# First experts' results stored by slot and gathered by token; six of eight images enter the third attention inside its steps

## The chip, the cores and the metric

The kernel runs on one core of a Trainium2 chip (trn2). Its engines work in parallel, each through its own instruction stream, and meet through semaphores: TensorE (PE: matrix products and transposes, results in PSUM), VectorE (DVE), ScalarE (ACT), GpSimd (POOL) and SyncE (SP), which here only issues transfers. GpSimd issues the indirect transfers (gathers and scatters of rows of 128 floats, one row per partition). The metric is the device time of one execution in microseconds; lower is better. Profiled executions give the trace.

## The reference

Eight images of 128 channels and 256 pixels pass through two convolutional attention layers, an attention (L2), a mixture of experts (L2), an attention (L3) and a mixture of experts (L3). What the change touches, cut to it (t is 8 images x 256 tokens x 128):

```python
t = t + _L2_ffn_ref(_ln_t(t), ...)     # first experts: 8 experts of 128 -> 512 -> 128, gelu, biases, top 2 of 8
t = t + _L3_attn_ref(_ln_t(t), ...)    # third attention: 8 heads of 16, 256 x 256 scores for each image and head
t = t + _L3_ffn_ref(_ln_t(t), ...)     # second experts: 8 experts of 128 -> 256 -> 128, silu(x w1) * (x w3), top 2

def _L2_ffn_ref(x, gate_w, gate_b, w1, b1, w2, b2):
    raw_weights = softmax(x @ gate_w + gate_b)
    top_w, top_idx = top_k(raw_weights, 2)
    expert_out = gelu(x @ w1[e] + b1[e]) @ w2[e] + b2[e]     # for each expert e
    return sum of expert_out[top_idx] * top_w                # for each token

def _L3_attn_ref(hidden_states, Wq, Wkv, Wo, bo):
    q, k, v = projections, 8 heads of 16
    scores = (q * scale @ k.T).astype(bfloat16)
    probs = softmax(scores)                                  # bfloat16
    out = (probs.astype(float32) @ v).astype(bfloat16)
    return out.astype(float32) @ Wo + bo
```

## The kernel before

The tokens t lie in SBUF as 128 partitions x (half s of the image, image b, 128 channels); N is 256 tokens of an image, T is 2048. Float32 operands of products are split into a high part (fp32r) made by ScalarE and a low part made by VectorE, and multiplied in three passes (xH*wH, xL*wH, xH*wL).

**First experts**, `experts(0, ...)`, one block of instructions (`nc.Block`; all five engines meet at its end). The router on VectorE and TensorE gives each of the 4096 pairs of token and expert a slot in 39 tiles of 128 rows (NT = 39), each tile of one expert. `pos` holds the slot of each pair; `slots`, `rows_of_slots` and `tables` turn this into `idx`, for each slot the row of the tokens' copy in DRAM (`rows_in`), and `places_aside` into `idy`, the row of `rows_out` where its result goes (rows of empty slots go to a place aside). GpSimd gathers tile j by `idx` into `xg` (`gather(j)`, six buffers), TensorE transposes and multiplies (`transposed`, `up`, `hidden_transposed`, `down`), ScalarE and VectorE evacuate, VectorE writes the result to `yo` (`result(j)`, L1479, three buffers), GpSimd scatters it by `idy` to `rows_out` (`scatter(j)`, L1109). GpSimd's order is: eight gathers, then scatter j and gather j + 8 in turn. After the last scatter has landed, SP fetches `rows_out` in token order into `both` (`fetch`, L946), one pair of images c at a time, two transfers per pair; pairs 0 and 1 in this block, 2 and 3 in the next. `both` is the same memory as `xc` (the first result of each token) and `lnT` (the second).

**Third attention**, `block4`. For each of four pairs of images: ScalarE scales the second results by their gates (`weighted_rows`), VectorE adds both to t (`combine`, L962 and L968), takes mean and variance (`measured`, L203, L208, L895), GpSimd raises the variance to -1/2 (`pair_pool`, L899), VectorE normalises (`pair_apply`, L906), TensorE transposes (`pair_transposes`, L917), ScalarE and VectorE make `xH` and `xL` (`pair_high` L923, `pair_low` L929), TensorE projects the values (`project_values`), ScalarE brings them to `v3f` (`values_out`), and GpSimd splits them into three bf16 parts (`split_values`, L1587 to L1593). All this for all pairs stands in front of, or inside, the first of 32 steps; a step (b, g) works on two of the eight heads of image b. The order inside a step is written out by hand for each engine and staggered: in step (b, g) TensorE makes the scores of three steps ahead, ScalarE rounds those of two steps ahead (`rounded`, L1618) and takes the exponentials of one step ahead (L1627), VectorE takes the maxima and subtracts them one step ahead (`centre`, L1818 to L1823), normalises the present ones (`normalise`, L1828, L1831), takes the low parts of a projection five fragments ahead (`lower`, L1810, L1812) and gathers outputs (L1846, L1854, L1859). `images` runs the steps: image 0 written out, images 1 to 5 as a loop, 6 and 7 written out. PSUM bank 0 (QKB) holds the projections of queries and keys in its two halves, and banks 4 to 7 the values and transposes of the start.

**Second experts**, `experts(1, ...)`: the same code with `hid` 256; its results go by scatter and fetch, and stay so.

## Time and profile before

| | |
|---|---|
| median of 3 runs | 623.33 us (623.15 to 624.60) |
| profiled execution | 623.73 us, span 621.9 us, mean granted clock 0.771 |
| PE / PEld busy | 503.7 us (81%) / 395.8 us (64%) |
| DVE busy | 433.9 us (70%) |
| ACT busy | 284.4 us (46%) |
| POOL busy | 286.1 us (46%) |
| first experts, from block to block | 161.9 to 306.06 us |
| third attention | 306.06 to 469.43 us |

A span is the time from the first to the last instruction of the trace; the device time holds 1.8 us more. Busy shares are means over stages with different limits, so they are read by stage. "PEclk" is the granted clock of TensorE as a share of 2.4 GHz: 0.50 is 1.2 GHz. A timeline row gives start, duration, engine, line and operation, out<-in, how many instructions are merged in it, and in brackets the idle time before it and what ended it.

### The profile page before, as it was taken

What the parts mean: (1) busy time and instruction counts of PE and PEld (TensorE: products, weight loads), DVE (VectorE), ACT (ScalarE), POOL (GpSimd) and SP (SyncE); (2) the same over time, 40 slices, a digit from 0 to 9 for tenths busy, and PEclk for the clock granted to TensorE, in tenths of its full rate; (3) what the DMA queues carried; (4) which work ended last, traced back from release to release, by engine and by line L of the source; (5) the groups of instructions that cost most, each with busy time, mean ns of one, the idle gap of its engine ahead of it and who ended that gap; (6) DMA issues with size and microseconds to landing.
All of it is one profiled execution on the core that took longest, in us unless ns stands there. A gap on an engine that the chain in (4) does not pass through costs nothing. (4 is left out here: it accounts for less than half of the span.)

```text
span 621.9 us, 10346 instructions
## 1 busy us (share of the span) xinstructions
PE 503.7 (81%) x3062; PEld 395.8 (64%) x3062; DVE 433.9 (70%) x1235; ACT 284.4 (46%) x754; POOL 286.1 (46%) x269
## 2 busy tenths in 40 slices
PE   9998995889667999999148899999857668777752
PEld 4785563859534999998147787777647346555531
DVE  2628559998876458544388799999997866555534
ACT  4523134400311764444236899999861023333324
POOL 1093438879344677775112111111112157777750
PEclk9698576999658999999665555555555799999995
DMA  6000070000550111212500000000004011112216
GB/s 226 1 1 2 0 271 0 1 1 1 188 150 26 49 52 52 52 53 43 147 1 2 1 2 0 0 0 0 1 2 114 22 35 51 52 52 51 51 48 199
DMA packets 26508, 31.06 MB, mean 50 GB/s; under 512 B 3105, under 2 KB 21538, under 8 KB 26338
## 3 DMA queue, kind: packets, MB, share of 16 engines
q1 hardware_dynamic: 21474, 20.29, 10.1%
q0 software_dynamic: 4992, 10.23, 6.4%
q8 instruction: 24, 0.39, 0.3%
q14 instruction: 18, 0.15, 0.1%
HBM read 20.16 MB, written 10.36 MB: 49 GB/s over the span
## 5 line engine op out<-in xcount | busy, mean ns | idle before, releaser
L1103 POOL DMA_INDIRECT xg<-rows_in,idx x78 | 76.5, 981 | 36.5 <-issue 21.6
L1109 POOL DMA_INDIRECT rows_out<-yo,idy x78 | 77.0, 988 | 31.8 <-issue 18.3
L1161 ACT ACTIVATE hraw<-ps 128x512 f32<-128x512 f32 (+1 forms) x78 | 38.3, 492 | 94.1 <-PE ps L1271 94.1
L1471 DVE TENSOR_TENSOR hidden<-ps,hidden 128x512 fp32r<-128x512 f32 (+1 forms) x78 | 43.3, 555 | 42.5 <-ACT hidden L1168 42.5
L1292 PE MATMUL ps<-wHL,hidden 128*128 x234 | 68.8, 346 | 0.6 <-DVE hidden L1471 0.4
L1295 PE MATMUL ps<-wHL,hidden 128*128 x234 | 53.9, 230 | 0.0
L1627 ACT ACTIVATE p<-s 128x256 bf16<-128x256 bf16 x128 | 51.6, 413 | 3.5 <-DVE s L1823 3.4
L1587 POOL CAST vp<-v3f 128x256 bf16<-128x256 f32 x8 | 3.6, 450 | 95.8 <-ACT s L1618 95.8
L1292 PEld LDWEIGHTS ps<-wHL,hidden 128*128 128x128 f32 x234 | 44.1, 189 | 2.9 <-issue 1.4
L1154 ACT ACTIVATE xa<-ps 128x128 fp32r<-128x128 f32 x78 | 21.9, 281 | 50.2 <-PE ps L1255 49.7
L1295 PEld LDWEIGHTS ps<-wHL,hidden 128*128 128x128 f32 x234 | 44.6, 191 | 0.0
L1269 PE MATMUL ps<-wHL,xa 128*128 x78 | 34.5, 443 | 10.6 <-issue 9.8
L1479 DVE TENSOR_REDUCE yo<-ps 128x128 f32<-128x256 f32 x78 | 32.6, 418 | 11.4 <-PE ps L1295 8.6
L1466 DVE TENSOR_TENSOR hraw<-hraw,ps 128x256 f32<-128x256 f32 x39 | 16.4, 422 | 33.0 <-ACT hraw L1161 33.0
L1168 ACT ACTIVATE hidden<-ps 128x512 fp32r<-128x512 f32 (+1 forms) x78 | 37.8, 485 | 1.5 <-PE ps L1279 1.5
L1279 PE MATMUL ps<-w,hraw 128*128 128x128 f32 x234 | 38.2, 272 | 0.3 <-DVE hraw L1466 0.3
L1279 PEld LDWEIGHTS ps<-w,hraw 128*128 128x128 f32 x234 | 30.2, 140 | 10.8 <-DVE hraw L1466 0.6
L1712 PE MATMUL ps<-identb,p 128*128 128x128 bf16 x256 | 33.3, 310 | 4.1 <-DVE p L1831 3.6
L763 PE MATMUL ps<-w,pw 128*128 128x128 f32 x256 | 30.7, 285 | 4.4 <-DVE pw L596 4.4
L763 PEld LDWEIGHTS ps<-w,pw 128*128 128x128 f32 x256 | 30.4, 201 | 5.4 <-issue 3.7
L1255 PE MATMUL ps<-w,xg 128*128 128x128 f32 x78 | 22.9, 293 | 13.4 <-DMA xg<-rows_in,idx 12.8
L1618 ACT ACTIVATE s<-ps 128x1024 bf16<-128x1024 f32 x32 | 32.8, 1024 | 1.7 <-PE ps L1701 0.3
(287 smaller groups left out, 1398.6 us busy)
## 6 DMA issues: line engine op xcount, KB each, us to landing
wraw<-in_ex SPq DMA_DIRECT2D x2, 2048.0 KB, 10.1
rows_in<-both SPq DMA_DIRECT2D x8, 512.0 KB, 5.9
both<-rows_out SPq DMA_DIRECT2D x16, 256.0 KB, 4.1
wraw<-in_ex SPq DMA_DIRECT2D x1, 3072.0 KB, 12.7
w<-in_pack SPq DMA_DIRECT2D x1, 1582.0 KB, 8.3
xg<-rows_in,idx POOLq DMA_INDIRECT x78, 2.6
rows_out<-yo,idy POOLq DMA_INDIRECT x78, 2.3
xs<-in_x SPq DMA_DIRECT2D x4, 256.0 KB, 4.6
```

What stands on the lines that cost most here:

```text
L763: x = pe.matmul(o, pw[:, q, k, :], ident, start=k == 0, stop=k == B - 1)
L1103: pool.indirect_dma_start(xg[:, j % NXG, :], None, xs_d[:], bass.IndirectOffsetOnAxis(idx[:, j:j + 1], 0)).then_inc(ld[j % NXG], 16)
L1109: pool.indirect_dma_start(ys_d[:], bass.IndirectOffsetOnAxis(idy[:, j:j + 1], 0), yo[:, j % NYO, :], None).then_inc(st[j % NYO], 16)
L1161: act.activation(hraw[:, j % 2, :], ps[:, HB + j % 2, 0:hid], ACT.Gelu if layer == 0 else ACT.Silu).then_inc(z["act"], 1)
L1168: act.activation(hH[:, j % 2, :], ps[:, HTB + j % 2, 0:hid], ACT.Copy).then_inc(z["hH"], 1)
L1269: pe.matmul(o, xa[:, j % NX, :], wh, start=layer == 1, stop=False)
L1279: x = pe.transpose(ps[:, HTB + j % 2, h * P:(h + 1) * P], hraw[:, j % 2, h * P:(h + 1) * P], ident)
L1292: pe.matmul(o.rearrange("p (i n) -> p i n", i=2), hH[:, j % 2, h * P:(h + 1) * P], both, start=h == 0, stop=False)
L1295: x = pe.matmul(o[:, 0:P], hL[:, j % 2, h * P:(h + 1) * P], wHL[:, bass.ds(e, 1), 0, cols].rearrange("p a n -> p (a n)"), start=False, sto ...
L1471: dve.tensor_tensor(hL[:, j % 2, :], ps[:, HTB + j % 2, 0:hid], hH[:, j % 2, :].bitcast(F32), ALU.subtract).then_inc(z["hL"], 1)
L1627: act.activation(p3[:, g % 2, r, :], s3[:, g % 2, r, :], ACT.Exp, accum_out=smb3[:, g, r:r + 1]).then_inc(m3["ex"], 1)
L1712: x = pe.transpose(psb(TB)[:, ((h * S + kt) * S + s) * P:((h * S + kt) * S + s + 1) * P], p3[:, g % 2, h * S + s, kt * P:(kt + 1) * P], id ...
```

## The change

First experts: `scatter` and `idy` are gone in this layer. VectorE copies `pos` to `slot_of`; SP stores each result tile as it is to `rows_by_slot`, in slot order; GpSimd issues all gathers of tokens, waits for all stores, and then gathers the results of image 0, four indirect transfers of 128 rows (`result_rows`: two halves of the image, two experts). The results of images 1 to 7 are gathered by GpSimd in the next block, four transfers an image.

Third attention: the work of the start is done image by image instead of pair by pair (`add_rows`, `scaled_rows`, `image_sum`, `image_apply`, `image_transposes`, `image_high`, `image_low`, `image_values`, `image_values_out`, `image_pool`). Images 0 and 1, and sum and normalisation of image 2, stand before the steps. The rest of image 2, and images 3 to 7, stand in the steps: with n = 4b + g, image i is summed in step n = 4i - 10, normalised one step later, transposed two, split into high and low part three, its values projected three and brought out four steps later (`coming`). The transposes and values use the half of bank 0 that the projection of the same step doesn't. `images` is written out in full, without a loop. The transfers of images 1 to 3 are mixed by hand on GpSimd with the powers of images 0 to 2 and the splitting of the values.

```diff
+        def image_pool(pool, b):
+            pool.wait_ge(c3["var"], b + 1)
+            pool.tensor_tensor(rstd[:, :, b], var[:, :, b], halfs[:, 0:S], ALU.pow).then_inc(c3["rst"], 1)
+
+        def image_sum(dve, b):
+
+            add_rows(dve, b)
+            ln_moments(dve, chv, range(S), (b,))
+            chv.wait()
+            dve.tensor_scalar(var[:, :, b], mv[:, :, b, 1], LN_EPS, None, ALU.add).then_inc(c3["var"], 1)
+
+        def image_apply(dve, b):
+
+            dve.wait_ge(c3["rst"], b + 1)
+            for s in range(S):
+                k = dve.tensor_scalar(xc[:, s, b, :], t[:, s, b, :], mv[:, s, b, 0:1], rstd[:, s, b:b + 1], ALU.subtract, ALU.mult)
+            k.then_inc(c3["nrm"], 1)
+
+        def image_columns(b):
+
+            return ps[:, 6 + b, 0:N] if b < 2 else ps[:, 0, N:2 * N]
+
+        def image_rows(b):
+
+            return ps[:, 6 + b, 0:N] if b < 2 else ps[:, 0, 0:N]
+
+        def image_transposes(pe, b):
+
+            pe.wait_ge(c3["nrm"], b + 1)
+            for s in range(S):
+                x = pe.transpose(image_columns(b)[:, s * P:(s + 1) * P], xc[:, s, b, :], ident)
+            x.then_inc(c3["tp"], 1)
+
+        def image_high(act, b):
+
+            act.wait_ge(c3["tp"], b + 1)
+            act.activation(xH[:, b * N:(b + 1) * N], image_columns(b), ACT.Copy).then_inc(c3["xh"], 1)
+
+        def image_low(dve, b):
+
+            dve.wait_ge(c3["xh"], b + 1)
+            cols = slice(b * N, (b + 1) * N)
+            dve.tensor_tensor(xL[:, cols], image_columns(b), xH[:, cols].bitcast(F32), ALU.subtract).then_inc(c3["xl"], 1)
+
+        def image_values(pe, b):
+
+            pe.wait_ge(c3["xl"], b + 1)
+            for s in range(S):
+                o, cols = image_rows(b)[:, s * P:(s + 1) * P], slice(b * N + s * P, b * N + (s + 1) * P)
+                pe.matmul(o, xH[:, cols], wv3H[:], start=True, stop=False)
+                pe.matmul(o, xL[:, cols], wv3H[:], start=False, stop=False)
+                x = pe.matmul(o, xH[:, cols], wv3L[:], start=False, stop=True)
+            x.then_inc(m3["vp"], 1)
+
+        def image_values_out(act, b):
+
+            act.wait_ge(m3["vp"], b + 1)
+            act.activation(v3f[:, b].rearrange("p s c -> p (s c)"), image_rows(b), ACT.Copy).then_inc(m3["vf"], 1)
...
+        def result_rows(pool, b, pieces=range(TOPK * S)):
+
+            for n in pieces:
+                k, s = n % TOPK, n // TOPK
+                r = row(0, s, b)
+                pool.indirect_dma_start(y_rows(k, s, b), None, yt_d[:],
+                                        bass.IndirectOffsetOnAxis(slot_of[:, k, r:r + 1], 0)).then_inc(gathered[b % NCH], 16)
+
+        def scaled_rows(act, b):
+
+            act.wait_ge(gathered[b % NCH], 16 * TOPK * S * (b // NCH + 1))
+            for s in range(S):
+                x = act.activation(y_rows(1, s, b), y_rows(1, s, b), ACT.Copy, scale=gk[:, row(0, s, b), 1:2])
+            x.then_inc(y_weighted, 1)
+
+        def add_rows(dve, b):
+
+            dve.wait_ge(gathered[b % NCH], 16 * TOPK * S * (b // NCH + 1))
+            for s in range(S):
+                x = dve.scalar_tensor_tensor(t[:, s, b, :], y_rows(0, s, b), gk[:, row(0, s, b), 0:1],
+                                             t[:, s, b, :], ALU.mult, ALU.add)
+            chv.done(x)
+            chv.wait()
+            dve.wait_ge(y_weighted, b + 1)
+            chv.done(dve.tensor_tensor(t[:, :, b, :], t[:, :, b, :], lnT[:, :, b * P:(b + 1) * P], ALU.add))
+            chv.wait()
...
-                for n in range(NYO):
-                    sp.wait_ge(st[n], st0[n] + 16 * len(range(n, NT, NYO)))
-                for c in range(NCH if layer == 1 else 2):
-                    fetch(sp, c)
-                if layer == 1:
+                if layer == 0:
+                    for j in range(NT):
+                        sp.wait_ge(z["yo"], j + 1)
+                        sp.dma_start(yt_d[j * TM:(j + 1) * TM], yo[:, j % NYO, :]).then_inc(kept[j % NYO], 16)
+                else:
+                    for n in range(NYO):
+                        sp.wait_ge(st[n], 16 * len(range(n, NT, NYO)))
+                    for c in range(NCH):
+                        fetch(sp, c)
...
-                pool.wait_ge(z["idy"], z0["idy"] + 1)
-                for j in range(NT):
-                    scatter(j)
-                    if j + NXG + 2 < NT:
-                        gather(j + NXG + 2)
+                if layer == 0:
+                    for j in range(NXG + 2, NT):
+                        gather(j)
+                    pool.wait_ge(z["dest"], 1)
+                    for n in range(NYO):
+                        pool.wait_ge(kept[n], 16 + 16 * len(range(n, NT, NYO)))
+                    result_rows(pool, 0)
+                else:
+                    pool.wait_ge(z["dest"], z0["dest"] + 1)
+                    for j in range(NT):
+                        scatter(j)
+                        if j + NXG + 2 < NT:
+                            gather(j + NXG + 2)
...
+                        dve.tensor_copy(slot_of[:], pos[:]).then_inc(z["dest"], 1)
...
-                places_aside()
+                if layer == 1:
+                    places_aside()
...
+        def images(step):
+
+
+            for b in range(B):
                 for g in range(4):
-                    step(b, g, False)
-            if around:
-                around(None)
-            for b in (B - 2, B - 1):
-                for g in range(4):
-                    step(b, g, False)
+                    step(b, g, b == 0)
...
+        def coming(b, g, late):
+
+            n = 4 * b + g - late + 10
+            return n // 4 if n % 4 == 0 and 2 <= n // 4 < B else None
...
-            pair_pool(pool, 0)
-            pair_pool(pool, 1)
-            pair_pool(pool, 2)
-            pair_pool(pool, 3)
...
+            result_rows(pool, 1, range(3))
+            image_pool(pool, 0)
+            result_rows(pool, 1, range(3, 4))
+            result_rows(pool, 2, range(2))
+            image_pool(pool, 1)
+            result_rows(pool, 2, range(2, 4))
             split_values(0)
-            for b in range(1, B):
-                pool.wait_ge(m3["sb"], 4 * b + 1)
-                split_values(b)
+            image_pool(pool, 2)
+            result_rows(pool, 3)
+            split_values(1)
+            for b in range(4, B):
+                result_rows(pool, b)
+                image_pool(pool, b - 1)
+                split_values(b - 2)
+            image_pool(pool, B - 1)
+            split_values(B - 2)
+            split_values(B - 1)
             for c in range(3):
-                pair_pool(pool, c, c4)
+                pair_pool(pool, c)
...
-            weighted_rows(act, 0, 0)
-            weighted_rows(act, 0, 1)
-            pair_high(act, 0)
+            scaled_rows(act, 0)
+            image_high(act, 0)
             for n in range(4):
                 upper(*fragment(0, 0, n), bank=n)
-            weighted_rows(act, 0, 2)
-            pair_high(act, 1)
-            weighted_rows(act, 0, 3)
-
-            def values_out(c, n):
-
-                act.wait_ge(m3["vp"], c + n)
-                act.activation(v3f[:, 2 * c:2 * (c + n)].rearrange("p b s c -> p (b s c)"), flat(ps[:, 4 + c:4 + c + n, :]), ACT.Copy).then_inc(m3["vf"], 1)
-
-            values_out(0, 2)
+            scaled_rows(act, 1)
+            image_values_out(act, 0)
             rounded(0, 0)
+            image_high(act, 1)
             rounded(0, 1)
             upper(*fragment(0, 0, 4))
-            pair_high(act, 2)
             exponentials(0, 0)
-            pair_high(act, 3)
+            image_values_out(act, 1)
+            scaled_rows(act, 2)
 
             def step(b, g, first):
+                if coming(b, g, 0):
+                    scaled_rows(act, coming(b, g, 0))
                 if there(*ahead(b, g, 2)):
                     rounded(*ahead(b, g, 2))
                 if g != 3 and not (first and g == 0):
                     evacuate(*((b, g - 1) if g else (b - 1, 3)))
                 if there(*fragment(b, g, 5)[:2]):
-                    upper(*fragment(b, g, 5))
+                    upper(*fragment(b, g, 5), high=coming(b, g, 3), rows=coming(b, g, 4))
                 if there(*ahead(b, g, 1)):
                     exponentials(*ahead(b, g, 1))
-                if first and g == 0:
-                    values_out(2, 1)
-                    values_out(3, 1)
-            images(act, step)
+            images(step)
...
-            pair_transposes(pe, 0)
+            image_transposes(pe, 0)
             pe.wait_ge(c3["xl"], 1)
             for n in range(4):
                 project(*fragment(0, 0, n), bank=n)
-
-            def project_values(c):
-
-                pe.wait_ge(c3["xl"], c + 1)
-                for i in range(4):
-                    o, cols = ps[:, 4 + c, i * P:(i + 1) * P], slice(c * CH + i * P, c * CH + (i + 1) * P)
-                    pe.matmul(o, xH[:, cols], wv3H[:], start=True, stop=False)
-                    pe.matmul(o, xL[:, cols], wv3H[:], start=False, stop=False)
-                    x = pe.matmul(o, xH[:, cols], wv3L[:], start=False, stop=True)
-                x.then_inc(m3["vp"], 1)
-
-            project_values(0)
-            pair_transposes(pe, 1)
-            project_values(1)
+            image_values(pe, 0)
             pe.wait_ge(m3["prl"], 4)
             scores(0, 0)
-            pe.wait_ge(m3["vf"], 1)
             scores(0, 1)
+            image_transposes(pe, 1)
+            pe.wait_ge(c3["xl"], 2)
             project(*fragment(0, 0, 4))
+            image_values(pe, 1)
             scores(0, 2)
-            pair_transposes(pe, 2)
             project(*fragment(0, 0, 5))
-            pair_transposes(pe, 3)
 
             def step(b, g, first):
                 if there(*ahead(b, g, 3)):
                     scores(*ahead(b, g, 3))
-                if first and g == 0:
-                    project_values(2)
-                    project_values(3)
                 if first and g == 1:
-                    pe.wait_ge(m3["vf"], 3)
+                    pe.wait_ge(m3["vf"], 2)
                 if not (first and g == 0):
                     values(*((b, g - 1) if g else (b - 1, 3)))
                 if g == 1 and not first:
@@ -1792,8 +1855,8 @@
                     final(b - 1)
                 transposed(b, g)
                 if there(*fragment(b, g, 6)[:2]):
-                    project(*fragment(b, g, 6))
-            images(pe, step)
+                    project(*fragment(b, g, 6), columns=coming(b, g, 2), rows=coming(b, g, 3))
+            images(step)
...
-            summed(0)
-            combine(dve, 0, 1)
-            pair_apply(dve, 0)
-            measured(1)
-            pair_low(dve, 0)
+            image_sum(dve, 0)
+            image_apply(dve, 0)
+            image_low(dve, 0)
             for n in range(4):
                 lower(*fragment(0, 0, n), bank=n)
-            pair_apply(dve, 1)
-            summed(2)
-            pair_low(dve, 1)
-            summed(3)
-            pair_apply(dve, 2)
+            image_sum(dve, 1)
+            image_apply(dve, 1)
+            image_low(dve, 1)
             centre(0, 0)
             lower(*fragment(0, 0, 4))
-            pair_low(dve, 2)
-            pair_apply(dve, 3)
+            image_sum(dve, 2)
+            image_apply(dve, 2)
 
             def step(b, g, first):
+                for late, work in ((0, image_sum), (1, image_apply)):
+                    if coming(b, g, late):
+                        work(dve, coming(b, g, late))
                 if there(*ahead(b, g, 1)):
                     centre(*ahead(b, g, 1))
-                if first and g == 0:
-                    pair_low(dve, 3)
-                if g == 3 and isinstance(b, int) and b == B - 1:
+                if g == 3 and b == B - 1:
                     finished(0)
                 if g == 3:
                     evacuate(b, 2)
                 normalise(b, g)
                 if there(*fragment(b, g, 5)[:2]):
-                    lower(*fragment(b, g, 5))
+                    lower(*fragment(b, g, 5), low=coming(b, g, 3))
```

## Rows read from the trace of the kernel before

**Rows 1.** Busy time by stage: start and steps of the third attention.
```profile
306.06:346.80 40.74, 26.08 (x143) 23.00 (x144) 30.24 (x112) 21.38 (x55) 6.30 (x8) 0.54 0.10 27
346.80:469.43 122.63, 108.03 (x862) 87.15 (x859) 118.46 (x421) 106.76 (x315) 19.55 (x31) 0.50 0.00 1
```

**Rows 2.** Timeline of VectorE in the first experts: results L1479.
```profile
206.30 0.41 DVE L1479 TENSOR_REDUCE yo<-ps 128x128 f32<-128x256 f32 x1
...
281.55 0.41 DVE L1479 TENSOR_REDUCE yo<-ps 128x128 f32<-128x256 f32 x1
...
284.50 0.42 DVE L1479 TENSOR_REDUCE yo<-ps 128x128 f32<-128x256 f32 x1 [0.36 <-PE ps L1295]
...
287.39 0.41 DVE L1479 TENSOR_REDUCE yo<-ps 128x128 f32<-128x256 f32 x1
```

**Rows 3.** Timeline of GpSimd: the first experts' end, the kernel's end.
```profile
284.03 0.97 POOL L1103 DMA_INDIRECT xg<-rows_in,idx  x1 [0.30 <-issue]
...
298.40 0.97 POOL L1109 DMA_INDIRECT rows_out<-yo,idy  x1 [0.40 <-DVE yo L1479]
...
602.57 0.97 POOL L1109 DMA_INDIRECT rows_out<-yo,idy  x1 [0.30 <-issue]
```

**Rows 4.** Source view of three block ends: ns min/median/max, first and last start.
```profile
L1510 POOLq DRAIN  x1: 7643/7643/7643, 298.2 to 298.2; - x1
...
L994 POOLq DRAIN  x1: 1112/1112/1112, 466.6 to 466.6; - x1
...
L1929 POOLq DRAIN  x1: 8204/8204/8204, 601.8 to 601.8; - x1
```

**Rows 5.** The page, DMA issues: line engine op xcount, us to landing.
```profile
xg<-rows_in,idx POOLq DMA_INDIRECT x78, 2.6
rows_out<-yo,idy POOLq DMA_INDIRECT x78, 2.3
```

**Rows 6.** Timeline, start of the third attention, all engines.
```profile
306.06 1.28 ACT L1604 ACT_TABLE_LOAD   x1 [10.49 <-PEq L1510]
306.11 1.14 DVE L962 SCALAR_TENSOR_TENSOR t<-both,gk,t 128x128 f32<-128x128 f32 x4 [7.98 <-PEq L1510]
307.35 2.44 ACT L954 ACTIVATE both<-both,gk 128x128 f32<-128x128 f32 x8
...
309.46 0.87 DVE L203 BATCH_NORM_STATS2 stats<-t 128x6 f32<-128x128 f32 x4
...
311.03 1.08 POOL L899 TENSOR_TENSOR rstd<-var,halfs 128x4 f32<-128x4 f32 x1 [11.66 <-DVE var L895]
...
312.75 1.11 DVE L906 TENSOR_SCALAR both<-t,mv,rstd 128x128 f32<-128x128 f32 x4
...
316.51 0.58 PE L1686 MATMUL ps<-xH,wq3H 128*128 128x256 f32 x1 [1.41 <-DVE xL L929]
...
319.89 0.48 DVE L1812 SCALAR_TENSOR_TENSOR k3S<-k3H,w,ps 128x256 fp32r<-128x256 f32 x1 [0.22 <-ACT k3H L1610]
```

**Rows 7.** Busy time of one image in the steady part of the steps.
```profile
389.60:405.40 15.80, 15.19 (x122) 12.39 (x120) 15.38 (x54) 14.72 (x45) 2.40 (x4) 0.50 0.00 0
```

**Rows 8.** Groups of VectorE in that image: busy us, mean ns.
```profile
L1831 DVE TENSOR_SCALAR p<-p,sm 128x256 bf16<-128x256 bf16 x17 | 4.1, 302 | 0.1
L1823 DVE TENSOR_SCALAR s<-s,mx 128x256 bf16<-128x256 bf16 x16 | 3.6, 291 | 0.1
...
L1859 DVE TENSOR_TENSOR t<-t,ps 128x256 f32 x1 | 0.4, 411 | 0.0
```

**Rows 9.** Timelines: VectorE beside GpSimd, in the first experts and the steps.
```profile
234.41 1.02 DVE L1495 TENSOR_TENSOR wHL<-wraw,wHL 128x768 fp32r<-128x768 f32 x1
234.44 0.97 POOL L1103 DMA_INDIRECT xg<-rows_in,idx  x1 [0.30 <-issue]
...
396.35 0.73 POOL L1589 TENSOR_TENSOR v3r<-v3f,vp 128x256 f32<-128x256 f32 x1
...
396.67 1.22 DVE L1831 TENSOR_SCALAR p<-p,sm 128x256 bf16<-128x256 bf16 x4
```

169 lines of the change are left out of this document (72 added, 97 removed).

## The prediction

> **What bounds the kernel now.** I read the views in this order: the page, for the shares of the engines; busy time by stage; the timeline of the end of the first experts and of the start of the third attention; the source view of each block's end; then the stages image by image. The page's chain of waits is of no use here: it starts at 469 us, behind everything that the diff touches.
>
> The stage view [rows 1] splits the third attention in two. The start (306.06 to 346.80, block start to the centring for step (0,3)) holds 30.2 us of VectorE in 40.7: latency with idle engines. The steps (346.80 to 469.43) hold 118.5 us of VectorE in 122.6. One image in the steady part shows 15.38 of 15.80 us busy on VectorE against 14.72 on ScalarE and 15.19 on TensorE at a granted clock of 0.50, the 1.2 GHz level [rows 7]. VectorE works without a pause; the missing 0.4 us is gaps of some 0.03 us between dependent instructions. So VectorE bounds the steps, and what is put on it there is paid in full. The change puts work there.
>
> In the first experts the results come 2.51 us apart (206.30 to 281.55 are 30 intervals), by TensorE, whose instructions stand there without a gap; then two come late, after 2.95 and 2.89 us [rows 2]; the last ends at 298.1, just ahead of the last scatter. GpSimd alternates gather and scatter, 0.97 us and 0.30 between, some 2.55 us a tile [rows 3]: nearly TensorE's 2.51, so it delays little.
>
> Between the last scatter's end (299.37 [rows 3]) and the attention's first instruction (306.06) GpSimd's DRAIN runs 7.6 us from 298.2 to 305.8 [rows 4]. The transfer itself lands 2.3 us after its issue, at 300.7 [rows 5]. The drain at the kernel's end does the same: from 601.8 for 8.2 us to 610.0, with the last scatter issued at 602.57 and finished at 603.54 [rows 3, 4]. Both end 6.5 us after the last indirect transfer's instruction. The drain behind the attention, where GpSimd's last work is a power, takes 1.1 us, as long as that power [rows 4, 6]. This start of the block is therefore set by "last indirect transfer plus 6.5 us", and the change puts four such transfers later.
>
> **The change, part by part.** All sums are against the profiled execution: 623.7 us (span 621.9), 0.4 above the median of 623.3.
>
> (a) First experts. The 39 scatters leave GpSimd; SP stores the tiles in order, one per 2.5 us, on a queue that is empty by then. Only the two late results can be won: 0.44 + 0.38 = 0.8 us. Three buffers of results cover a store's landing (2.3 us against 7.5 us of tiles), and gathers run at most six buffers ahead. The table idy and its five small VectorE instructions fall behind the first gather, where VectorE waits anyway: nothing. The copy into slot_of stands in front of it: about 0.1 us; it is one small instruction between two others, and 0 and 0.3 (an addition on eight times as many elements takes 0.41 [rows 8]) bound it. Net -0.7: last result at 297.4.
>
> (b) The boundary. Before: scatter, landing, SP's fetches, the drain beside them. After: the last store must land (no such store is in the trace; 64 KB by scatter take 2.3 us, and I take that; 2.0 to 2.6 as bounds): 299.8, GpSimd starts at 300.0. Four gathers for image 0 at 1.27 us: the last begins at 303.8 and ends at 304.8; it lands 2.6 us after its issue [rows 5], 306.4, under the drain. The drain ends 6.5 us behind, 311.3, and all five engines start the block at 311.5 instead of 306.06: **+5.4**. All engines stand behind this barrier; nothing covers it.
>
> (c) The start of the attention, from the block's first instruction. Before, the first projection came 10.45 us in (316.51), behind a combination of two pairs; it comes 3.2 us sooner now [rows 6]. In order: table load 1.28 and two scalings at 0.3, to 1.9; the rest of the sum (add 0.42, statistics 0.44, aggregation 0.2, variance), to 3.3. GpSimd has first to issue three gathers (3.8 us), so the power runs from 4.2 to 4.95 (0.75; four values take 1.08). Two normalisations 0.56, transposes 0.6, high part 0.4, low part 0.4, each with 0.1 of handover: projection at 7.25. The last lower part of the first four ends 3.86 us later, as before (316.51 to 320.37 [rows 6]): 11.1. Then image 1, in sequence and no longer under other work: sum 1.9, power 1.0, normalisation 0.6, transposes to low part 1.5: 16.1. Centring 2.1 and one lower part 0.4: 18.6. Sum of image 2: its scaled rows stand in ScalarE's queue behind the exponentials (18.2 to 19.9), the values (0.4) and take 0.6, so the sum ends at 22.3; power and normalisation: 24.0. Step (0,0) 3.4, step (0,1) 3.4 and image 2's low part 0.4: centring for (0,3) could start at 31.5. Before it stood at 40.7 [rows 1]. **-9.2.** The gathers of images 1 and 2 land in time: GpSimd issues them by 6 and 16 us in.
>
> (d) The steps. Per image, pairs halved [rows 6], add and low part by the 0.41 of a 128x256 addition [rows 8]: two scaled additions 0.56, addition 0.42, statistics 0.44, aggregation 0.21, variance 0.08, four gaps 0.15: 1.86; normalisation 0.56; low part 0.42. Five sums, five normalisations and five low parts (images 3 to 7) fall in: 9.3 + 2.8 + 2.1 = **+14.2**. ScalarE gets 1.4 us an image (14.7 to 16.1) and TensorE some 1.8 at this clock, both inside the new period of about 18.6. GpSimd needs 8.4 us an image (four gathers, power, values) and is two steps ahead.
> (e) GpSimd beside VectorE. Where a GpSimd addition overlaps, four VectorE scalings take 1.22 us instead of 0.87 [rows 9], 0.35 us lost to an image's 2.4 us of GpSimd work [rows 7]; with another 0.14 for the subtractions just before them, seen at the same place, 0.2 per us. Five more powers of 0.75: +0.8. For the 20 gathers issued in the steps (19.4 us) the two ends are 0 (the 128x768 subtraction takes 0.95 to 1.02 us under gathers and scatters [rows 9]) and 0.2 x 19.4 = 3.9. I take 1.0, nearer to the row that has the same GpSimd instruction. **+1.8.**
>
> The Trainium skill (SBUF — State Buffer, Who interferes with whom) has it that a VectorE instruction in a 2-port mode and a GpSimd instruction exclude each other for the whole instruction. The slow scalings [rows 9] agree with that for tensor instructions. No row shows it for descriptor writing, and by that rule the sum would end up at the second rival's time.
>
> Sum: +5.4 - 9.2 + 14.2 + 1.8 = +12.2; 623.7 + 12.2 = 635.9, and 0.4 lower as a median: **635.5 us**. The same from VectorE's side: its work in the attention rises from 148.7 by 8 x 0.3 for splitting pairs and 1.8, its idle time in the start stays near 10 us, since each image's chain now runs bare.
>
> **The rivals.**
> *The drain is not repeated.* If the 6.5 us belong to scatters or overlap with what came before, the block starts at 305.0 and image 0 is in at 306.4; its scaled rows and sum then run 0.9 us sooner than before the change. For it: only scatters were ever last. Against: two drains with the same remainder and transfers of the same kind. 623.7 - 0.9 - 9.2 + 14.2 + 1.8 - 0.4 = 629 us.
> *Gathers block VectorE.* If each gather holds VectorE's bf16 instructions (4.1 + 3.6 of 15.8 us, 49% [rows 8]) for its whole 0.97 us, 19.4 x 0.49 = 9.5 us take the place of the 1.0: 644 us. Against: the 0.95 to 1.02 of the subtractions [rows 9].
> *Faster: the steps hide the moved work.* If VectorE's queue had room, a share h of 16.0 us (14.2 + 1.8) would vanish: 5.4 - 9.2 + 16.0 x (1 - h). It decides from h = 0.76 on; wholly hidden it gives 619.5 us. Against: 0.42 us of idle VectorE an image [rows 7], 2.1 us over five images, h = 0.13 at most.
> That the first experts gain more, because the scatters were the bound, is excluded by TensorE's 2.51 us [rows 2], which stay.
>
> **How the numbers follow.** The forecast as summed has 0.62 (632 to 639), the drain not repeated 0.17 (around 629), blocking gathers 0.10 (up to 644), hidden work 0.07 (around 620), the rest 0.04, near no change. The range leaves out the hidden case and most of the blocking one: 628.5 to 641. A measurement of this kernel can tell 0.3%, 1.9 us, from no change. Faster by more 0.07, within 0.04, slower 0.89.
>
> **What would show it.** (a) Results 2.51 us apart throughout, the last some 0.7 us sooner. (b) GpSimd's drain ending 6.5 us behind the fourth gather of image 0, and the attention's table load at about 311.5; at 305 the first rival holds. (c) First projection 7 us behind the block's start, step (0,3) centring about 33 us behind it with image 3's sum before it. (d) 18.6 us per image in steps of images 1 to 4 instead of 15.8, VectorE still 97% busy, and 15.9 for images 6 and 7. (e) VectorE's bf16 scalings no longer than 0.35 us beside gathers; 0.6 or more speaks for blocking. The prediction is wrong if the drain costs nothing, or if the period grows by less than 2 us an image.

## The result and the profile after

The kernel after takes **635.25 us** (median of 4 runs, 634.2 to 638.35) against 623.41 before: a ratio of 1.0191, 95% interval 1.0167 to 1.0215, so 11.8 us slower. The forecast was 635.5. The profiled execution took 635.91 us (span 634.0), 12.2 more than that of before.

I split this difference at the same three places in both traces: the first instruction of the attention's block, the centring for step (0,3), the end of the last addition to t.

| stretch | predicted | measured |
|---|---|---|
| last result of the first experts | -0.7 (inside the next line) | -0.7 |
| start of the attention's block | +5.4 | +2.15 (306.06 to 308.21) |
| block start to centring for (0,3), image 3's sum in it | -9.2 + 1.9 = -7.3 | -6.8 (40.74 to 33.96) |
| from there to the last addition | 14.2 - 1.9 + 1.8 = +14.1 | +15.4 (122.6 to 138.0) |
| from there to the second experts | 0 | +0.5 (0.32 to 0.84) |
| second experts | 0 | +0.8 |

The rows add to 12.1, the difference of the spans; the -0.7 is part of the +2.15. The last two rows have to be read together. From the last addition to the end of the trace it is 152.45 us before and 153.83 us here. In five other kernels with the same code behind the attention and the same or a later second boundary (e_next, e_more, a_drain, e_scale, e_nosum, all below) it is 152.4 to 152.7 us. So these 1.4 us belong mainly to this execution, and no other run shows that the later boundary reaches the kernel's end. Up to the last addition the change costs 10.7 us; two of the four runs (634.2 and 634.59) are 10.8 and 11.2 above the median before.

Busy time of the two stretches of the attention and of one image in the steps (window: length, then busy us and instructions of PE, PEld, DVE, ACT, POOL, then clock, DMA share, GB/s), the answer to [rows 1, 7]:

```profile
308.21:342.17 33.96, 17.68 (x111) 15.12 (x112) 22.39 (x77) 19.14 (x52) 20.71 (x26) 0.55 0.10 25
342.17:480.17 138.00, 109.57 (x891) 89.03 (x890) 131.05 (x468) 109.06 (x326) 34.05 (x46) 0.52 0.03 9
361.44:380.89 19.45, 14.72 (x119) 12.31 (x119) 18.55 (x65) 15.77 (x48) 6.92 (x9) 0.55 0.05 14
```

VectorE stands still for 11.6 us of the start (10.5 before [rows 1]) and is busy for 131.05 of 138.0 in the steps. Its idle time there has grown from 4.2 to 7.0 us. An image takes 19.45 us; VectorE works in 18.55 of them. Behind the moved work nothing got slower: the last additions to t (L1924) come 15.0, 13.6 and 5.7 us apart, before 15.5, 13.6 and 5.7.

First experts, results on VectorE (answer to [rows 2]), and GpSimd's end (answer to [rows 3]):

```profile
206.44 0.41 DVE L1560 TENSOR_REDUCE yo<-ps 128x128 f32<-128x256 f32 x1
...
281.64 0.41 DVE L1560 TENSOR_REDUCE yo<-ps 128x128 f32<-128x256 f32 x1
...
284.15 0.41 DVE L1560 TENSOR_REDUCE yo<-ps 128x128 f32<-128x256 f32 x1
...
286.65 0.41 DVE L1560 TENSOR_REDUCE yo<-ps 128x128 f32<-128x256 f32 x1
...
296.96 0.42 DVE L1560 TENSOR_REDUCE yo<-ps 128x128 f32<-128x256 f32 x1 [0.95 <-PE ps L1373]
```

```profile
273.18 0.94 POOL L1173 DMA_INDIRECT xg<-rows_in,idx  x1 [1.56 <-PE ps L1333]
299.69 0.94 POOL L1033 DMA_INDIRECT both<-rows_by_slot,slot_of  x1 [25.57 <-DMA rows_by_slot<-yo]
...
303.44 0.94 POOL L1033 DMA_INDIRECT both<-rows_by_slot,slot_of  x1 [0.30 <-issue]
```

The two late results are gone (284.15 and 286.65 are 2.51 and 2.50 behind their predecessors; before 2.95 and 2.89). GpSimd has nothing to do from 274 to 299.7, then issues image 0's four gathers and ends at 304.38. The blocks' ends, source view (duration min/median/max in ns, first and last start), the answer to [rows 4]:

```profile
L1591 POOLq DRAIN  x1: 7130/7130/7130, 300.8 to 300.8; - x1
```

```profile
L1060 POOLq DRAIN  x1: 3411/3411/3411, 477.3 to 477.3; - x1
```

The first drain ends at 307.93, **3.55 us** behind the last gather's end, not 6.5. The second, at the end of the attention, ends at 480.71, 2.3 us behind the end of GpSimd's last power (478.37). Before, that one ended with its power [rows 4]. It is late now and sets the start of the second experts: the +0.5.

The start, on the path of image 0, all engines, the answer to [rows 6]:

```profile
308.21 1.28 ACT L1684 ACT_TABLE_LOAD   x1 [13.39 <-PEq L1591]
...
309.51 0.69 ACT L1040 ACTIVATE both<-both,gk 128x128 f32<-128x128 f32 x2
...
310.30 0.43 DVE L1052 TENSOR_TENSOR t<-t,both 128x256 f32<-128x256 f32 x1 [1.43 <-ACT both L1040]
...
312.30 0.74 POOL L909 TENSOR_TENSOR rstd<-var,halfs 128x2 f32<-128x2 f32 x1
...
313.07 0.66 DVE L922 TENSOR_SCALAR both<-t,mv,rstd 128x128 f32<-128x128 f32 x2 [1.34 <-POOL rstd L909]
...
315.47 0.58 PE L1765 MATMUL ps<-xH,wq3H 128*128 128x256 f32 x1 [0.93 <-DVE xL L949]
```

The first projection comes 7.26 us behind the block's start; 7.25 was predicted. The power follows GpSimd's third gather without a pause, so the gathers do stand in front of it.

In the steps, VectorE's addition of the second rows, L1052, of images 4 to 7 (in brackets the idle time before it and its releaser):

```profile
360.10 0.43 DVE L1052 TENSOR_TENSOR t<-t,both 128x256 f32<-128x256 f32 x1 [0.49 <-ACT both L1040]
...
379.55 0.43 DVE L1052 TENSOR_TENSOR t<-t,both 128x256 f32<-128x256 f32 x1 [0.38 <-ACT both L1040]
...
399.29 0.43 DVE L1052 TENSOR_TENSOR t<-t,both 128x256 f32<-128x256 f32 x1 [0.66 <-ACT both L1040]
...
418.69 0.42 DVE L1052 TENSOR_TENSOR t<-t,both 128x256 f32<-128x256 f32 x1 [0.38 <-ACT both L1040]
```

and ScalarE at the second of them:

```profile
378.35 0.43 ACT L1711 ACTIVATE p<-s 128x256 bf16<-128x256 bf16 x1
378.66 0.21 ACT L1711 ACTIVATION_READ_ACCUMULATOR p<-s 128x1 bf16 x1
378.75 0.70 ACT L1040 ACTIVATE both<-both,gk 128x128 f32<-128x128 f32 x2
```

At each of these images VectorE waits for a scaling that stands in ScalarE's queue behind four exponentials: 1.9 us in the four rows. The engine that bounds the steps waits for one that doesn't. The prediction has no such wait.

### The profile page after: what moved, and what is told of

Read it like the earlier page. It is cut to its first block and busy times, and to the rows that moved or that the text cites. A ratio compares the mean times of both kernels' runs of the same rounds, so it can differ in the third digit from the quotient of the medians.

```text
span 634.0 us, 10030 instructions
## 1 busy us (share of the span) xinstructions
PE 500.6 (79%) x3062; PEld 392.4 (62%) x3062; DVE 438.2 (69%) x1243; ACT 284.2 (45%) x763; POOL 278.2 (44%) x266
## 5 line engine op out<-in xcount | busy, mean ns | idle before, releaser
L1173 POOL DMA_INDIRECT xg<-rows_in,idx x78 | 74.8, 958 | 69.0 <-PE ps L1333 40.9
L1033 POOL DMA_INDIRECT both<-rows_by_slot,slot_of x32 | 31.3, 979 | 38.3 <-DMA rows_by_slot<-yo 25.6
L1179 POOL DMA_INDIRECT rows_out<-yo,idy x39 | 38.4, 985 | 14.5 <-issue 10.1
L1560 DVE TENSOR_REDUCE yo<-ps 128x128 f32<-128x256 f32 x78 | 32.6, 418 | 12.3 <-PE ps L1373 8.4
L1791 PEld LDWEIGHTS ps<-identb,p 128*128 128x128 bf16 x256 | 24.7, 140 | 24.9 <-DVE p L1896 24.8
L1357 PEld LDWEIGHTS ps<-w,hraw 128*128 128x128 f32 x234 | 30.3, 141 | 11.2 <-DVE hraw L1547 0.8
L556 PE MATMUL ps<-w 128*128 128x512 f32 x50 | 33.9, 841 | 0.3 <-PEq L516 0.3
```

The lines of the kernel that those rows point to most:

```text
L556: pe.matmul(ps[:, bank, :], ident, w[:, 0:CH], start=True, stop=True)
L1173: pool.indirect_dma_start(xg[:, j % NXG, :], None, xs_d[:], bass.IndirectOffsetOnAxis(idx[:, j:j + 1], 0)).then_inc(ld[j % NXG], 16)
L1179: pool.indirect_dma_start(ys_d[:], bass.IndirectOffsetOnAxis(idy[:, j:j + 1], 0), yo[:, j % NYO, :], None).then_inc(st[j % NYO], 16)
L1357: x = pe.transpose(ps[:, HTB + j % 2, h * P:(h + 1) * P], hraw[:, j % 2, h * P:(h + 1) * P], ident)
L1791: x = pe.transpose(psb(TB)[:, ((h * S + kt) * S + s) * P:((h * S + kt) * S + s + 1) * P], p3[:, g % 2, h * S + s, kt * P:(kt + 1) * P], id ...
```

## The experiments

Three questions were open: what GpSimd's drain costs, what the 15.4 us of the steps are made of, and whether the gathers take anything from VectorE. Beside them I tried to win from the kernel before what the change had wanted to win. "Block start" is always the first instruction of the attention, "attention" the time from there to the end of the last addition.

**e_fetch**: the second half of the change alone. The first experts scatter and fetch as before; the attention is that of after, without gathers.

```diff
-                if layer == 0:
-                    for j in range(NT):
-                        sp.wait_ge(z["yo"], j + 1)
-                        sp.dma_start(yt_d[j * TM:(j + 1) * TM], yo[:, j % NYO, :]).then_inc(kept[j % NYO], 16)
+                for n in range(NYO):
+                    sp.wait_ge(st[n], st0[n] + 16 * len(range(n, NT, NYO)))
+                if layer == 0:
+                    for c in range(2):
+                        fetch(sp, c, gathered)
...
+        @block4.sync
+        def _(sp):
+            for c in range(2, NCH):
+                fetch(sp, c, gathered)
...
             for b in range(4, B):
-                result_rows(pool, b)
                 image_pool(pool, b - 1)
```

> The second half of the change alone: images enter the attention as in the changed kernel, but the first experts scatter by token and SP fetches, as before the change. My theory (VectorE bounds the steps and pays for all that is put there; gathers cost it little): block start back at 306.1 (-2.1 us), GpSimd free for the first power (-0.3), some 1 us less beside gathers: 632 us, period per image still about 19 us. Rival (gathers hold VectorE's fast instructions): 8 to 9 us less in the steps, 624 us, period near 17.5.

Measured: 632.24 us, ratio 1.0139 (1.0092 to 1.0185). Block start 305.99, and the attention as long as with 28 gathers in it:

```profile
306.04:478.24 172.20, 126.16 (x1000) 103.23 (x1000) 153.33 (x543) 127.91 (x377) 26.56 (x43) 0.54 0.03 7
```

After:

```profile
308.21:480.17 171.96, 127.25 (x1000) 104.15 (x1000) 153.44 (x543) 128.20 (x377) 54.77 (x71) 0.53 0.04 12
```

VectorE is busy 153.33 us without and 153.44 us with them. By the first instruction of the block, at 305.99, the attention lasts 172.25 us here and 171.96 in the kernel after. So the attention's loss (8.6 us, from 163.4) comes with the image-by-image work, and taking the gathers out gives nothing back. In the start the first projection comes 6.71 us in, 0.55 sooner than behind three gathers, but the next two normalisations take 1.14 us instead of 0.60, with GpSimd's splitting of the values beside them:

```profile
319.37 1.14 DVE L922 TENSOR_SCALAR both<-t,mv,rstd 128x128 f32<-128x128 f32 x2 [0.82 <-POOL rstd L909]
```

The centring for (0,3) comes 34.1 us in, and 34.0 us in the kernel after. The profiled executions of the two kernels are 3.3 us apart: 2.2 are the earlier block start, 1.3 lie behind the last addition (152.49 against the 153.83 that only that execution shows), and -0.3 in the attention.

**e_nogather**: after without the gathers of images 4 to 7, whose results are left out (the memory holds other rows there).

```diff
             for b in range(4, B):
-                result_rows(pool, b)
                 image_pool(pool, b - 1)
```

> The changed kernel without the 16 gathers of images 4 to 7 (their results are left out; all arithmetic stays and works on what lies in the tiles). My theory: 16 gathers cost VectorE 0 to 0.2 us each, 632 to 635 us, most likely 634. Rival (a gather holds VectorE): -7 to -8 us, 628 us. Rival (the in-step waits are waits for gathered rows): the idle time of VectorE before the addition of the second rows goes.

Measured: 634.03 us, ratio 1.0158 (1.012 to 1.0195). The attention lasts 172.1 us, as long as with the gathers. The boundary behind it is back at 0.32 us, and the stretch behind the last addition lasts 152.7 us all the same. Its drain:

```profile
L1060 POOLq DRAIN  x1: 2102/2102/2102, 477.7 to 477.7; - x1
```

It ends 1.03 us behind the last power (477.76 + 1.01), with 12 gathers issued in the block; after has 28 gathers and 2.34 us, before none and nothing. The last transfer of this block was issued more than 100 us earlier. So the drain's cost is not about a transfer that is still on its way, and it grows with their number.

**e_next**: image 0's gathers moved behind the block's end.

```diff
-                    for n in range(NYO):
-                        pool.wait_ge(kept[n], 16 + 16 * len(range(n, NT, NYO)))
-                    result_rows(pool, 0)
...
+            for n in range(NYO):
+                pool.wait_ge(kept[n], 16 + 16 * len(range(n, NT, NYO)))
+            result_rows(pool, 0)
             result_rows(pool, 1, range(3))
```

> The changed kernel with image 0's four gathers moved behind the block's end, so that no indirect transfer stands close before GpSimd's drain. My theory: the drain is short, the block starts at about 298, the gathers run from 299.7 to 304.4, the last lands at 305.9, the table load is hidden under them, and the attention runs 3.5 us sooner: 631.7 us. Rival (the drain costs several us whatever stands before it): the block starts at 301 to 304, the gathers come behind it, and the time is 635 to 638 us.

Measured: 630.78 us, ratio 1.0121 (1.0077 to 1.0165). The block starts at 298.06, since the first drain lies under TensorE's last tiles (273.0 to 278.3). The gathers start at 299.62 all the same, as the stores land then, but no drain stands behind them: image 0's power runs at 308.20 instead of 312.30. The drain at the other end, with 32 gathers in its block, ends 2.65 us behind the last power, and the second experts start 1.17 us behind the last addition; the kernel still ends 152.4 us behind that addition.

**e_more**: does each transfer count? Sixteen more gathers into spare memory, issued while GpSimd is idle.

```diff
                     pool.wait_ge(z["dest"], 1)
+                    for n in range(16):
+                        pool.indirect_dma_start(y_rows(n % 2, (n // 2) % 2, 4 + n // 4), None, xs_d[:],
+                                                bass.IndirectOffsetOnAxis(idx[:, n:n + 1], 0)).then_inc(gathered[3], 16)
+                    pool.wait_ge(gathered[3], 256)
```

> The kernel after with 16 more indirect gathers in the first experts' block: GpSimd issues them between its last gather of tokens and its wait for the stores, where it stands idle for over 20 us, from the tokens' copy into memory of images 4 to 7 that nothing reads before it is written again. They end long before the four gathers of image 0. Theory (the drain costs 0.082 us for each indirect transfer issued since the last drain, read from five kernels): 59 transfers instead of 43, so the drain ends 4.85 us behind the last gather instead of 3.55, the attention's block starts at 309.5 us instead of 308.2, and the profiled time is 637.2 us. Rival (the drain waits for the last transfer to land, or costs a fixed time): block start 308.2 and 635.9 us as in the kernel after.

Measured, one execution: 636.28 us. GpSimd's last gathers and the drain:

```profile
293.41 0.95 POOL L1196 DMA_INDIRECT both<-rows_in,idx  x1 [0.30 <-issue]
299.93 0.95 POOL L1033 DMA_INDIRECT both<-rows_by_slot,slot_of  x1 [5.58 <-DMA rows_by_slot<-yo]
...
303.68 0.94 POOL L1033 DMA_INDIRECT both<-rows_by_slot,slot_of  x1 [0.30 <-issue]
```

```profile
L1595 POOLq DRAIN  x1: 8440/8440/8440, 301.1 to 301.1; - x1
```

The drain ends at 309.54, 4.92 us behind the last gather (4.85 expected; 3.55 in the kernel after). The spare gathers had landed, and GpSimd had waited for that, before the last four were issued; the last of them was issued 6.5 us ahead of those. They still cost some 1.4 us at the block's end (4.92 - 3.55), 0.08 to 0.09 us each. The attention starts at 309.76. The time of 637.2 that I had expected was 0.9 too high: it was counted from the execution of after with its 1.4 us behind the attention.

**a_drain**: does a drain in the middle take the cost away? One drain instruction in GpSimd's idle time.

```diff
                     pool.wait_ge(z["dest"], 1)
+                    pool.drain()
                     for n in range(NYO):
```

> The kernel after with one GpSimd drain instruction between its last gather of tokens and its wait for the stores, in the first experts alone. Theory (cost per transfer since the last drain): this drain takes 39 x 0.082 = 3.2 us where GpSimd is idle anyway, and the one at the block's end has 4 transfers left, 0.3 us, or waits for the last gather to land (2.6 us after its issue at 303.4, so 306.0). The attention's block starts at 304.9 to 306.2 instead of 308.2 and the kernel takes 632.3 to 633.5 us. Rival (the block's end is fixed by the last transfer or by all transfers of the block): start at 308.2, 635.3 us.

Measured: 633.47 us, ratio 1.0156 (1.0131 to 1.0181), 1.8 us below the kernel after. In the profiled execution everything up to here is 3.5 us late already, so only differences inside it say something:

```profile
307.01 0.95 POOL L1033 DMA_INDIRECT both<-rows_by_slot,slot_of  x1 [0.31 <-issue]
```

```profile
L1592 POOLq DRAIN  x1: 5294/5294/5294, 304.4 to 304.4; - x1
```

It ends at 309.69, 1.73 us behind the last gather's end instead of 3.55: the 1.8 us. With four transfers the count gives 0.3. What is left is about the landing: the transfer was issued at 307.01 and takes 2.5 to 2.6 us. The drain in the middle ended 4.5 us behind the 39th gather of tokens, more than the 3.2 expected.

**b_drain**: the same in the kernel before, behind the last gather of tokens, in both experts.

```diff
                     if j + NXG + 2 < NT:
                         gather(j + NXG + 2)
+                    if j + NXG + 2 == NT:
+                        pool.drain()
```

> The kernel before with one GpSimd drain instruction behind the last gather of tokens, in both experts; eight scatters follow it. Theory (cost per transfer since the last drain): the drain takes 70 x 0.082 = 5.7 us in the middle of the scatters. Three buffers of results cover some 4 us of it, so the results stall by 1 to 3 us, and GpSimd catches up at 1.27 us a scatter. At the block's end 8 transfers are left (0.7 us), and the last scatter lands 2.3 us after its issue: the first block's end comes some 2 to 5 us sooner, the kernel's end likewise, 615 to 620 us in all against 623.4. Rival (a drain in the middle clears nothing): both stalls are added and nothing is won, 625 to 629 us.

Measured: 628.59 us, ratio 1.0077 (1.0053 to 1.0101). Results on VectorE in the first experts:

```profile
289.75 0.41 DVE L1481 TENSOR_REDUCE yo<-ps 128x128 f32<-128x256 f32 x1
...
295.55 0.42 DVE L1481 TENSOR_REDUCE yo<-ps 128x128 f32<-128x256 f32 x1 [3.20 <-DMA rows_out<-yo,idy]
...
300.23 0.43 DVE L1481 TENSOR_REDUCE yo<-ps 128x128 f32<-128x256 f32 x1 [1.71 <-DMA rows_out<-yo,idy]
```

```profile
L1512 POOLq DRAIN  x1: 2801/2801/2801, 300.7 to 300.7; - x1
L1512 SPq DRAIN  x1: 122/122/122, 305.3 to 305.3; - x1
```

The drain in the middle takes 5.9 us behind its last scatter, near the 5.7 computed. It stands behind 39 gathers and 32 scatters, 71 transfers, and seven scatters follow it; my 70 and eight were one off. The three buffers fill, and the last result comes 2.5 us late. The drain at the block's end falls to 1.6 us. But the block starts at 305.7, only 0.4 us sooner: SP, which waits for the last scatter and then issues the fetches, is now the last at the barrier. In the second experts nothing comes back at all, and from their start to the end it takes 158.1 us instead of 152.1: the kernel's end hangs on the last scatter and what follows it on other engines, not on GpSimd's drain, which before ended 12 us ahead of it. The theory of the drain held, the forecast of the time (615 to 620 us) failed, and the time is that of the rival: I had not asked who is next at either end.

**e_scale**: the scaling of images 3 to 7 in front of the exponentials of the step before.

```diff
             def step(b, g, first):
-                if coming(b, g, 0):
-                    scaled_rows(act, coming(b, g, 0))
...
+                if coming(b, g, -1):
+                    scaled_rows(act, coming(b, g, -1))
                 if there(*ahead(b, g, 1)):
                     exponentials(*ahead(b, g, 1))
```

> The changed kernel with ScalarE scaling the second results of images 3 to 7 one step sooner, ahead of the exponentials. VectorE idles 0.4 to 0.7 us before that addition in each image. If this wait is a cost of its own: -2.0 to -2.5 us, 633 us. Rival (VectorE is not the bound there, or the scaling now delays the exponentials as much): 635 us.

Measured: 632.58 us, ratio 1.0137 (1.0099 to 1.0175), 2.7 us below after by the medians; the attention lasts 169.7 us instead of 172.0. The additions have no wait any more and come 18.87 us apart on the mean of four (L1052 from 340.90 to 416.36), in the kernel after 19.47 (340.83 to 418.69):

```profile
377.73 0.60 DVE L1047 SCALAR_TENSOR_TENSOR t<-both,gk,t 128x128 f32<-128x128 f32 x2
378.37 0.42 DVE L1052 TENSOR_TENSOR t<-t,both 128x256 f32<-128x256 f32 x1
...
396.93 0.60 DVE L1047 SCALAR_TENSOR_TENSOR t<-both,gk,t 128x128 f32<-128x128 f32 x2
397.57 0.43 DVE L1052 TENSOR_TENSOR t<-t,both 128x256 f32<-128x256 f32 x1
```

**e_nosum**: after without the addition of the rows of images 3 to 7 on VectorE, so that the tokens of these images lack the first experts' results.

```diff
             dve.wait_ge(gathered[b % NCH], 16 * TOPK * S * (b // NCH + 1))
+            if b >= 3:
+                return
             for s in range(S):
```

> The kernel after with the addition of the rows of images 3 to 7 left out on VectorE (three instructions an image, and the wait for ScalarE's scaled rows among them); gathers, scaling, statistics and all behind it stay. The output lacks these images' results of the first experts. Theory (VectorE is the bound of the steps and waits for the scaling): five images lose 0.30 + 0.30 + 0.42 us of additions with their handover and 0.4 to 0.5 us of wait, 1.5 us each, 7.6 us in all: 627.7 us. Rival (TensorE or ScalarE is the bound of the steps by now): at most the wait and a little more is won, 633 us or over.

Measured: 626.05 us, ratio 1.0048 (1.0032 to 1.0065). The last addition ends at 471.49, block start 308.18:

```profile
471.07 0.42 DVE L1926 TENSOR_TENSOR t<-t,ps 128x256 f32<-128x256 f32 x1 [0.21 <-PE ps L1828]
```

The attention loses 8.7 us, 1.7 an image; the instructions left out and their wait are 0.60 + 0.43 + 0.1 + 0.48, 1.6. That is more than the 1.5 an image that I had expected. What is taken from VectorE comes back in full: it bounds the steps, and neither TensorE nor ScalarE takes over within these 1.7 us.

**b_order**: in the start of the kernel before, VectorE has one large pause. It waits there for ScalarE's high part of a projection, which TensorE makes behind `project_values(3)`. I moved these products behind the projection.

```diff
                 if first and g == 0:
                     project_values(2)
-                    project_values(3)
...
                     project(*fragment(b, g, 6))
+                if first and g == 0:
+                    project_values(3)
```

> The kernel before with project_values(3) moved behind project(6) in step (0,0) on TensorE. In the start of the attention of the kernel before VectorE stands idle 3.5 us (342.9 to 346.5) until TensorE, which multiplies the values of the last pair of images at that time, has made the transposes or scores that it waits for. Theory (what the start costs is TensorE's order, not that all images stand in it): up to 3.5 us less, 620 to 622 us. Rival (the values are needed as soon as they are, or the wait moves on by as much): 623.4 us.

Measured: 624.69 us, ratio 1.0025 (1.0016 to 1.0034): slower by 1.3 us. The pause, before:

```profile
346.45 0.42 DVE L1810 SCALAR_TENSOR_TENSOR q3L<-ps,q3H 128x256 fp32r<-128x256 f32 x1 [3.51 <-ACT q3H L1610]
```

and now:

```profile
348.14 0.42 DVE L1811 SCALAR_TENSOR_TENSOR q3L<-ps,q3H 128x256 fp32r<-128x256 f32 x1 [5.03 <-ACT q3H L1610]
```

with ScalarE in front of it:

```profile
345.40 0.60 ACT L1648 ACTIVATE v3f<-ps 128x512 f32<-128x512 f32 x1 [3.48 <-PE ps L1763]
345.90 1.02 ACT L1618 ACTIVATE s<-ps 128x1024 bf16<-128x1024 f32 x1
346.80 1.03 ACT L1634 ACTIVATE pT<-ps 128x1024 bf16<-128x1024 bf16 x1
347.71 0.40 ACT L1610 ACTIVATE q3H<-ps 128x256 fp32r<-128x256 f32 x1
```

The projection was made 2.4 us sooner, but ScalarE's order was left as it was: `values_out(3, 1)` stands there ahead of the rounding and of this high part, and it waits for the moved products, 1.7 us later than before. The order of one engine was changed without its partner's. Moving both was not tried.

**b_pre**: the kernel before with the table load, and scaling and addition of images 0 and 1, in the first experts' block, under GpSimd's drain.

```diff
@@ experts, layer 0, end of ScalarE's part
+                    act.preload_act_table(ACT.Exp)
+                    weighted_rows(act, 0, 0)
@@ experts, layer 0, end of VectorE's part
+                    combine(dve, 0, 0)
@@ block4
-            act.preload_act_table(ACT.Exp)
-            weighted_rows(act, 0, 0)
-            summed(0)
+            measured(0)
```

> The kernel before with the load of the table of exponentials, the scaling of images 0 and 1 and their addition moved from the start of the attention's block to the end of the first experts' block, where ScalarE and VectorE only wait for the drain. Theory (until 306 us both engines are free and the fetched rows are there by then): the table load (1.28 us) and part of the sum leave the path, 1.5 to 3 us less, 620.5 to 622 us. Rival (the fetched rows land too late, so the block's end moves back by the time of the sum): 623 to 624 us.

Measured: **621.11 us**, ratio 0.9963 (0.9949 to 0.9976): faster than both kernels.

```profile
296.35 1.28 ACT L1184 ACT_TABLE_LOAD   x1
305.37 1.28 ACT L954 ACTIVATE both<-both,gk 128x128 f32<-128x128 f32 x4 [7.74 <-DMA both<-rows_out]
307.96 1.28 ACT L954 ACTIVATE both<-both,gk 128x128 f32<-128x128 f32 x4 [1.32 <-PEq L1515]
...
316.49 0.42 DVE L1813 SCALAR_TENSOR_TENSOR q3L<-ps,q3H 128x256 fp32r<-128x256 f32 x1 [1.52 <-ACT q3H L1614]
```

and the same projection before:

```profile
317.97 0.42 DVE L1810 SCALAR_TENSOR_TENSOR q3L<-ps,q3H 128x256 fp32r<-128x256 f32 x1 [1.51 <-ACT q3H L1610]
```

The fetched rows of images 0 and 1 land at 305.4, so the sum itself could start only 0.7 us sooner, and the next block now waits for it and starts at 307.96, 1.9 us later. But the table load is off the path, and the first lower part of a projection comes at 316.49 instead of 317.97. These 1.5 us are little more than the table load's 1.28; how much the early sum adds was not measured by itself. In this execution the last result of the first experts came 0.8 us later than before, and it is the slowest of the five.

**b_both**: the two edits together.

> The two edits to the kernel before together (project_values(3) behind project(6); table load and sum of images 0 and 1 in the first experts' block). If both hold, they add, as they shorten different stretches: 617.5 to 621 us. If one covers the other, the better of the two alone.

Measured: 622.71 us, ratio 0.9986 (0.9975 to 0.9997), 1.6 us above b_pre alone and outside both expectations: b_order costs about as much here as by itself (1.3).

**a_both**: the kernel after with the edits of e_next and e_scale.

> The kernel after with two edits that gained alone: image 0's gathers in the attention's block (630.8 us alone) and the scaling of images 3 to 7 one step sooner (632.6 us alone). They touch different stretches: 4.5 us before the start and 2.2 to 2.7 us in the steps, so 628 to 628.6 us together. It stays above 623.4, since the added instructions on VectorE in the steps are still there. Rival (the two overlap): 630.5 us.

Measured: 628.51 us, ratio 1.0086 (1.0071 to 1.0101). The gains nearly add: 4.5 and 2.7 us would give 628.05. Some 5 us above the kernel before are left, and the last addition of the attention ends 4.4 us later than before. I put them down to the work on VectorE; no run here shows that by itself.

## Why the prediction was right, and where it was not

The sign was right, and so was the mechanism: VectorE bounds the steps, and images moved into the steps are paid there in full, while the start gives back less. That the time agrees within 0.3 us is luck. The boundary was 3.3 us too high in the forecast. Against that the start came out 0.5 and the steps 1.3 us longer than forecast, and 1.3 us lie behind the attention, which no other kernel shows.

**(a) First experts**, -0.7: right. No slack was hidden in the scatters.

**(b) The boundary**, +5.4: the step that failed in its size. It measured +2.15. Stores landing (first gather at 299.7, predicted 300.0) and the four gathers (last end 304.4, predicted 304.8) were right within 0.4 us; the drain was not. I took "6.5 us behind the last indirect transfer" from two drains that agreed, and both had 78 transfers in front of them [rows 3, 4]. The two rows could not tell a fixed time from one that goes by the count. The change took 39 scatters out of that block and left 43 transfers: 3.55 us. By the same count the attention's own drain became late, +0.5 at the second boundary, where I had nothing; whether any of it reaches the end is not shown. The first rival (drain not repeated, 629 us) lies as far off on the other side: its block start was 305.0.

**(c) The start**, -9.2, or -7.3 with image 3's sum: measured -6.8. The chain of image 0 was right to 0.01 us. (The terms behind it, 24.0 + 3.4 + 3.4 + 0.4, make 31.2 and not 31.5.)

**(d), (e) The steps**, 14.2 - 1.9 + 1.8 = +14.1: measured +15.4. VectorE's added busy time is 12.6 us (118.5 to 131.05), with 12.3 forecast in (d), gaps included, and 1.8 in (e). Its idle time grew by 2.8 us, where I had none (it is 95% busy in the image shown above, not 97%): I costed the addition as instructions and didn't ask where its input stands in ScalarE's queue. e_scale shows that wait to be worth 2.3 us of the attention, 2.7 of the medians. The forecast's second count, from VectorE's side, could have warned me: 4.2 us more work and an idle time in the start near 10 give 4.2 us more attention, but the sum had 6.8, so it held 2.6 us more idle time than I wrote down. Measured are 4.7 us more work and 3.9 us more idle time.

(e) came out near its size. A bf16 scaling or subtraction of VectorE (L1888, L1896) takes 0.282 us in the steps where GpSimd does nothing. The time above that, over all 236 of them and split by what GpSimd did at the same time:

| kernel | beside gathers alone | beside GpSimd's arithmetic | together |
|---|---|---|---|
| before | none | 3.4 us | 3.4 us |
| after | 1.0 us (27 instructions) | 3.9 us | 4.9 us |
| e_fetch | none | 4.8 us | 4.8 us |
| e_nogather | none | 4.9 us | 4.9 us |

So the 1.0 us that I gave to the gathers is there, and +1.5 together against the +1.8 forecast. But it doesn't go with the gathers: without them more of GpSimd's arithmetic falls beside these instructions, and the attention stays as long (172.25 us without any, 172.1 without those of images 4 to 7, 171.96 with all). Period of an image: 18.6 predicted, 19.4 to 19.7 measured, 18.87 once the scaling comes in time.

**The rivals.** Blocking gathers (644 us) is refuted by e_fetch and e_nogather. Of the 27 instructions that run beside gathers alone, 17 take no more than 0.29 us, ten take 0.32 to 0.47 us, and none is held for a gather's 0.94 us. By the rule of the Trainium skill (SBUF — State Buffer, Who interferes with whom), an instruction of VectorE in a 2-port mode and one of GpSimd exclude each other for the whole instruction; for the gathers the trace shows no such hold, and no row shows which mode these instructions ran in. Hidden work (619.5 us) is refuted by e_nosum: 1.6 us taken off VectorE an image bring 1.7.

What stays open: the 1.4 us behind the attention in the profiled execution of after, and why the later second boundary doesn't lengthen the other kernels.

## What to carry to other kernels

Work moved out of a stage of latency into a stage whose engine is full is paid there in full; look first for what can be moved to where an engine waits anyway, as the table load under the drain (b_pre). Where an engine's order is written by hand, an instruction that moves takes its place in two queues: who makes its input, and who empties its output, has to move too (e_scale gained by it, b_order lost by leaving it out). And a cost read from two equal cases is one point, not two: ask what differs in the kernel after, here the number of transfers.

## What the runs showed of the hardware

GpSimd's drain at a block's end takes time for each indirect transfer that GpSimd has issued since its last drain, also for those that landed long ago. Time from the end of GpSimd's last instruction to the end of the drain, by the trace's unrounded times (above, the starts of the drains are rounded to 0.1 us):

| transfers since the last drain | us | where |
|---|---|---|
| 0 | 0.07 | before, end of the attention |
| 12 | 1.06 | e_nogather, end of the attention |
| 28 | 2.37 | after, end of the attention |
| 32 | 2.69 | e_next, end of the attention |
| 43 | 3.58 | after, first experts |
| 59 | 4.89 | e_more, first experts |
| 71 | 5.87 | b_drain, drain in the middle |
| 78 | 6.44 | before, both experts |

That is 0.07 us and 0.082 us for each transfer, within 0.03 us over the whole range. Every transfer here moves 128 rows, so the runs can't tell a cost of each transfer from one of each row. Four drains lie above the line. Two have few transfers, 4 (1.75 us, a_drain) and 7 (1.6 us, b_drain), and end 0.2 and 0.3 us behind the landing of the last one. Two follow at once on the 39th gather of tokens (4.25 us in e_next, 4.5 us in a_drain; 3.3 by the line); the extra 1.0 to 1.2 us there are not explained.
